# Picked pairs, feature products and prologue of a graph-and-expert kernel: products issued in halves, bias as three bfloat16 parts, zero rows by transfers, first lists per tile

## The reference, cut to what matters

```python
def _graph_conv_max(x, src, dst, W_rel, b, W_root):
    agg = jax.ops.segment_max(x[src], dst, num_segments=N)
    agg = jnp.where(jnp.isfinite(agg), agg, 0.0)
    return agg @ W_rel.T + b + x @ W_root.T
...
    h = jax.nn.relu(_graph_conv_max(x, src, dst, W1_rel, b1, W1_root))
    h = jax.nn.relu(_graph_conv_max(h, src, dst, W2_rel, b2, W2_root))
...
    x = x + _L0_gnn_ref(_layernorm(x, axis=-1), edge_index, ...)
    x = x + _L0_ffn_ref(_layernorm(x, axis=-1)[None], ...)[0]
```

## Time and profile before

| what | value |
|---|---|
| median of 3 runs | 1110.98 us (1107.28 to 1113.2) |
| the profiled execution, its own time | 1114.74 us |
| its span, first to last instruction | 1112.9 us |
| busy share: PE, DVE, POOL, ACT | 70%, 65%, 56%, 25% |
| granted PE clock, mean | 0.86 of full |

### The profile page before, as it was taken

One profiled execution on the slowest core, in us unless ns is written; L12 is line 12 of the kernel. 1 busy time (PEld: TensorE's weight loads), 2 busy tenths in 40 slices (PEclk: granted clock), 3 DMA queues, 4 the chain that ended last, 5 costly groups with the idle time before them and its releaser, 6 DMA issues.

```text
span 1112.9 us, 14709 instructions
## 1 busy us (share of the span) xinstructions
PE 779.7 (70%) x3119; PEld 438.7 (39%) x3119; DVE 719.8 (65%) x1428; ACT 278.6 (25%) x527; POOL 619.3 (56%) x609
## 2 busy tenths in 40 slices
PE   0248148888888779757128898878788686958497
PEld 0133013333333333222016656646456463726243
DVE  4949848568655866681466765765757566657767
ACT  0274332213231222001002233223223131313132
POOL 6540365355545655761777777777777777720012
PEclk9869569899988889888567999989989788978889
DMA  4830666575556566757667888888887878855874
GB/s 129 287 109 1 237 181 184 166 222 155 159 178 210 154 188 213 210 161 255 195 194 209 289 255 274 256 263 246 274 276 237 262 236 257 271 169 204 331 313 173
DMA packets 116373, 238.75 MB, mean 215 GB/s; under 512 B 53464, under 2 KB 57836, under 8 KB 112475
## 3 DMA queue, kind: packets, MB, share of 16 engines
q0 software_dynamic: 46080, 149.94, 43.4%
q1 hardware_dynamic: 54536, 40.85, 12.2%
q10 hardware_dynamic: 15730, 47.66, 11.5%
HBM read 201.28 MB, written 42.63 MB: 219 GB/s over the span
## 4 chain that ended last, share of the span: by engine, by line
PE 21%; DVE 21%; DMA 20%; issue 17%; POOL 10%; ACT 4%; DVEq 3%; ACTq 3%; POOLq 2%; SPq 0%
DMA mem<-tab,ic 13%; POOL mem L828 9%; PE pp L1154 6%; DMA ic<-idxf 4%; PE prow L1074 4%; PE pl L1101 3%; DVE mem L1456 2%; DVE weights L895 2%; DVE acc L949 2%; DVE acc L884 2%; PE prow L1088 1%; PE prow L1072 1%; DVE mem L562 1%; PE prow L1064 1%; PE pp L1121 1%
## 5 line engine op out<-in xcount | busy, mean ns | idle before, releaser
L828 POOL DMA_INDIRECT mem<-tab,ic x524 | 542.9, 1036 | 278.7 <-issue 144.2
L949 DVE TENSOR_TENSOR acc<-acc,mem 128x512 f32<-128x512 f32 x338 | 223.2, 694 | 165.7 <-SPq L791 156.2
L1121 PEld LDWEIGHTS pp<-xnT,weights 128*128 128x128 f32 x1280 | 159.3, 205 | 9.8 <-issue 9.8
L884 DVE TENSOR_TENSOR acc<-acc,pp 128x1024 f32<-128x1024 f32 x90 | 109.5, 1217 | 77.9 <-PE pp L1154 75.1
L1121 PE MATMUL pp<-xnT,weights 128*128 128x128 f32 x1280 | 159.8, 288 | 0.0
L1132 PE MATMUL pp<-weights,mem 128*128 128x512 f32 x320 | 142.6, 593 | 0.9 <-ACT mem L1292 0.9
L1154 PE MATMUL pp<-weights,LT 128*128 128x512 bf16 x300 | 77.0, 409 | 51.8 <-ACT idxf L699 34.9
L895 DVE TENSOR_TENSOR weights<-weights,mem 128x1024 f32<-128x1024 f32 x83 | 101.8, 1227 | 8.5 <-DVE weights L895 5.8
L1154 PE MATMUL pp<-weights,slots 128*128 128x512 bf16 x300 | 73.0, 392 | 23.1 <-DVE acc L884 23.1
L1088 PE MATMUL prow<-weights,aggT 128*128 128x512 f32 x152 | 82.6, 694 | 8.5 <-ACT aggT L1250 7.8
L1273 ACT ACTIVATE mem<-pp,b1T 128x128 f32<-128x128 f32 x160 | 45.6, 368 | 168.3 <-PE pp L1121 163.6
(11 more groups left out here) (305 smaller groups left out, 849.6 us busy)
## 6 DMA issues: line engine op xcount, KB each, us to landing
yd<-mem ACTq DMA_DIRECT2D x20, 1024.0 KB
weights<-yd SPq DMA_DIRECT2D x10, 2048.0 KB, 10.5
mem<-tab,ic POOLq DMA_INDIRECT x524, 3.9
weights<-in_L_ffn_W SPq DMA_DIRECT2D x9, 512.0 KB, 9.4
weights<-in_L_ffn_W ACTq DMA_DIRECT2D x7, 512.0 KB, 4.9
LT<-ttd ACTq DMA_DIRECT2D x5, 640.0 KB, 7.0
slots<-ttd ACTq DMA_DIRECT2D x5, 640.0 KB, 7.7
ic<-idxf SPq DMA_DIRECT2D x175, 1.0 KB
```

The lines of the kernel that those rows point to most:

```text
L828: g.indirect_dma_start(rings[l][:, j, :], None, table, bass.IndirectOffsetOnAxis(ic[:, j:j + 1], 0)).then_inc(s_gather[j], 16)
L884: v.tensor_tensor(acc[:, :, :], acc[:, :, :], pp[j % 2][:, :, :], ALU.max).then_inc(S["pa"], 1)
L949: v.tensor_tensor(acc[:, side, :], acc[:, side, :], rings[l][:, bass.ds(r % SLOTS, 1), :].rearrange("p a d -> p (a d)"), ALU.max).then_inc ...
L1121: ins = t.matmul(ph[w % 2][:, b * P:b * P + P], w1s[:, e, c, f * P:f * P + P], xnT[:, c, :], start=c == 0, stop=c == C - 1)
```

## The change

1. In layer 1, `root_product` is split: its transposes stand alone (`root`), and its product and `next_root_product` come in halves of two feature chunks, with one pair between the halves. `neighbours_product` comes after pair 6 instead of after pair 4.
2. The biases, formerly a float32 row times a row of ones, are cut into three bfloat16 parts by POOL (one cast and one subtraction in turn), laid on three partitions by three POOL DMAs, and added by one bfloat16 matmul.
3. POOL's memset of `hot`'s partitions 96 to 127 goes; partitions 125 to 127 are written by four transfers of the ACT queue at the start.
4. DVE's moments of `x` come after the ranks instead of before.
5. PE no longer waits for ACT's last instruction of the prologue, and SP loads the first index columns after the first of the ten lists (POOL still waits for all ten).

```diff
+        brow = acc[0:1, :, :]
+        bias3, ones3 = sb("bias3", [3, 2, D], BF16), sb("ones3", [3, P], BF16)
...
+        after(a, cg, n_neg)
+        zeros = zrow.bitcast(BF16).unsqueeze(1)
+        a.dma_start(hot[CN:CN + 1, :, 0, :], negrow.unsqueeze(1).to_broadcast([1, NC, D])).then_inc(S["neg"], 16)
+        a.dma_start(hot[CN:CN + 1, :, 1:3, :].rearrange("p c w d -> p c (w d)"), zeros.to_broadcast([1, NC, 2 * D]))\
+            .then_inc(S["neg"], 16)
+        for r in range(CN + 1, P):
+            a.dma_start(hot[r:r + 1, :, :, :].rearrange("p c w d -> p (c w d)").rearrange("p (i d) -> p i d", d=2 * D),
+                        zeros.to_broadcast([1, 3 * NC // 2, 2 * D])).then_inc(S["neg"], 16)
...
         for q in range(NQ):
+            if q == NQ - 1:
+                g.wait_ge(S["small"], 64)
             g.indirect_dma_start(big_rows[:, q, :], None, dstf,
...
-        after(g, cg, cg.n)
-        n_hot0 = cg.do(g.memset(hot[96:P, :, :, :], 0.0))
+        cg.do(g.memset(ones3[:, :], 1.0))
+        cg.link(g.tensor_copy(bparts[0], brow))
+        cg.link(g.tensor_tensor(brow, brow, bparts[0], ALU.subtract))
+        cg.link(g.tensor_copy(bparts[1], brow))
+        n_bias = cg.link(g.tensor_tensor(bparts[2], brow, bparts[1], ALU.subtract))
+        for i in range(3):
+            g.dma_start(bias3[i:i + 1, :, :], bparts[i]).then_inc(S["bias"], 16)
...
-        v.wait_ge(S["x"], 64)
-        cv.link(v.memset(mv[:, :, :], 1.0))
-        for q in range(NQ):
-            cv.do(v.bn_stats(st[0:CN, q, :], big_x[0:CN, q, :]))
...
+        v.wait_ge(S["x"], 64)
+        cv.link(v.memset(mv[:, :, :], 1.0))
+        for q in range(NQ):
+            n = cv.do(v.bn_stats(st[0:CN, q, :], big_x[0:CN, q, :]))
...
-        after(t, ca, ca.n)
         after(t, cv, n_meta)
         after(t, ca, n_low[NC - 1])
-        t.wait_ge(S["neg"], 16)
+        t.wait_ge(S["neg"], 64)
+        t.wait_ge(S["bias"], 48)
...
-            after(s, ca, n_idxf if l else n_idx1)
+            after(s, ca, n_idxf if l else n_idx1s[0])
...
                 def pe_tile(q, u):
                     pairs(q, u, (0, 1))
-                    root_product(q - 1)
+                    root(q - 1)
                     pairs(q, u, (2,))
+                    root_product(q - 1, (0, 1))
+                    pairs(q, u, (3,))
+                    root_product(q - 1, (2, 3))
                     neighbours(q - 1)
-                    pairs(q, u, (3, 4))
+                    pairs(q, u, (4, 5, 6))
                     neighbours_product(q - 1)
-                    pairs(q, u, (5, 6))
+                    pairs(q, u, (7,))
                     next_root(q - 1)
-                    pairs(q, u, (7, 8, 9))
-                    next_root_product(q - 1)
+                    pairs(q, u, (8,))
+                    next_root_product(q - 1, (0, 1))
+                    pairs(q, u, (9,))
+                    next_root_product(q - 1, (2, 3))
```

More of the change, by code:

```diff
@@ L221, in build @@
             ob oe od gd bn rc hs nmx exp apart_s warm apart_g apart_v x2l y out
-            neg bits pairs pa ga merge""".split()
+            neg bits bias pairs pa ga merge""".split()
         S = {n: sem("s_" + n) for n in names}
@@ L431, in build @@
         after(a, cg, n_neg)
-        after(a, cg, n_hot0)
-        a.dma_start(hot[CN:CN + 1, :, 0, :], negrow.unsqueeze(1).to_broadcast([1, NC, D])).then_inc(S["neg"], 16)
         after(a, cv, n_mean)
@@ L784, in build @@
                     .then_inc(S["fw"], 16)
+            else:
+                after(s, ca, n_idx1)
             def landed(i, h):
@@ L1065, in four, with root, root_product @@
                 ins.then_inc(S[event], 1)
-            def root_product(q):
+            def root(q):
                 t.wait_ge(S["rin"], q + 1)
                 four(pt0, xin, "rT")
-                t.wait_ge(S["rTe"], q + 1)
-                t.matmul(pg, ones[0:1, :], brow[0:1, 0, :], start=True, stop=False)
-                for c in range(C):
+            def root_product(q, cs):
+                if cs[0] == 0:
+                    t.wait_ge(S["rTe"], q + 1)
+                    t.matmul(pg, ones3[:, :], bias3[:, 0, :], start=True, stop=False)
+                for c in cs:
                     t.matmul(pg, rootT[:, c, :], wroot[0][:, c, :], start=False, stop=False)
@@ L1094, in next_root, with next_root_product @@
                 four(pt1, hst, "hT")
-            def next_root_product(q):
-                t.wait_ge(S["hTe"], q + 1)
-                t.matmul(pl[:, :], ones[0:1, :], brow[0:1, 1, :], start=True, stop=False)
-                for c in range(C):
+            def next_root_product(q, cs):
+                if cs[0] == 0:
+                    t.wait_ge(S["hTe"], q + 1)
+                    t.matmul(pl[:, :], ones3[:, :], bias3[:, 1, :], start=True, stop=False)
+                for c in cs:
                     ins = t.matmul(pl[:, :], xnT[:, c, :], wroot[1][:, c, :], start=False, stop=c == C - 1)
-                ins.then_inc(S["rp"], 1)
+                if cs[-1] == C - 1:
+                    ins.then_inc(S["rp"], 1)
             def ffn(q, between):
@@ L1174, in build @@
                 pe_tile(NQ - 1, 1)
-                root_product(NQ - 1)
+                root(NQ - 1)
+                root_product(NQ - 1, range(C))
                 neighbours(NQ - 1)
@@ L1178, in build @@
                 next_root(NQ - 1)
-                next_root_product(NQ - 1)
+                next_root_product(NQ - 1, range(C))
             else:
```

7 lines of the change are left out of this document (5 added, 2 removed).

## The result

The kernel with the change took 1075.91 us (median of 4 runs, 1074.5 to 1077.1), the kernel before 1111.32 us (1107.28 to 1113.2, its three runs and a fourth taken beside the change). The ratio is 0.9686, with a 95% interval of 0.9656 to 0.9716. The prediction was 1073 us within 1057 to 1091. On some chips single executions of one kernel differ by over 1.5%; ratios and intervals are taken from those that lie within that of the fastest, and where too few were left no ratio is given.

The account below looks back on a forecast made before the run. No engine is full (PE 70%), so waits decide, chiefly DVE's 74.4 us for pairs on PE. Terms -6.6, -7.5, -20.4, -3.6 sum to -38.1: 1114.74 becomes 1076.6, or 1073 us against the median, range 1057 to 1091.

Parts of the forecast that it names:

- tile 0, with the lists: Layer 1's first tile: earlier index columns and no PE wait for ACT's last list, less gather limits and cold start; -7.5 us.
- tiles 1 to 9: Layer 1: third pair waits for nothing, short waits remain at pairs 3, 4, 9; 54 us of waits for 74.4, -20.4 us.
- tail: After tile 9: root product and bias run bare, `xin` 2.0 us sooner, bias 0.4 instead of 2.05; -3.6 us.
- The key: Prologue, DVE's L363: without the memset it shortens by up to 8.6 us, less 2 for POOL's bias work; gain 6.6.
- What is late next is PE: Prologue: PE's transposes of the counts end at 104.5 instead of 106.06, so L588 moves from 111.30 to about 104.7.
- The lists: Tile 0: index columns loaded after the first list let POOL's first gather start at 139.2 instead of 141.51; 2.3 us.
- (a): Rival, layer 1: waits only move, both halves run at 1.2 GHz, tiles 1 to 9 gain next to nothing; 1093 us, chance 0.17.
- (b): Rival, prologue: POOL's bias work holds DVE as the memset did, until 37 us, so no gain there; 1080 us, chance 0.08.
- (c): Rival: all waits go and DVE runs through in tiles 1 to 9 and the prologue; 1055 us, chance 0.08.
- (d): Rival, slower: PE kept at 1.2 GHz becomes the bound, 54 us a tile against 36.4; 1250 us, chance 0.03.
- (e): Rival: POOL still waits for the tenth list and something unseen holds PE as before, no change; 1109 us, chance 0.02.
- The risk named for tiles 6 to 9: Sign of being wrong: DVE waits for SP's gathers in place of PE; 186 gathers need 232 of some 350 us.

Follow-up runs that it names:

- The kernel with the early copy: Changed kernel with ACT copying the next tile's `xin` at the end of the tile before, ahead of its wait for the root product: 1073.26 us, ratio 0.9636.
- the order alone: Kernel before with only PE's new order of layer 1, float32 bias kept; on three slower chips: 1296.53, 1294.75, 1288.84 us, third ratio 0.9835.
- the last experiment: Changed kernel with early `xin` copy, whole root product before pair 2, whole next root product before pair 7; three slower chips: 1279.31, 1273.38, 1268.23 us.

## Why the prediction was right, point by point

The prologue ends here with the last list (138.97 before, 135.06 with the change); its 3.9 us and 0.3 for the lists make the 4.2 by which the first fold came sooner.

| part | predicted | bounds | measured |
|---|---|---|---|
| prologue | -6.6 | -3 to -8.6 | -3.9 |
| tile 0, with the lists | -7.5 | -4 to -10.4 | -6.7 |
| tiles 1 to 9 | -20.4 | -36.6 to +2.1 | -23.9 |
| tail | -3.6 | -2 to -4 | -2.5 |
| layer 2 and last stage | 0 | -3 to +3 | -3.3 |
| sum | -38.1 | | -40.2 |

The sum is off by 2 us against the profiled executions and by 2.7 against the medians (35.4 us for 38.1), less than its parts are. The prologue, the lists and the tail fell short by 2.7, 2.0 and 1.1 us; tiles 1 to 9 and the rest of tile 0 gave 3.5 and 1.2 more, and layer 2 with the last stage 3.3 that was not forecast. That these cancel is luck; the mechanism in layer 1, which is the largest part, was right.

**The key** was right: 6.3 us instead of 6.6, and POOL held it for one instruction. I had allowed 2 us for that, and 2.3 were lost: the key took 1.97 us where its neighbours take 0.17, and L372 ahead of it 0.67 instead of 0.17. The prediction quoted the Trainium skill ("GPSIMD Engine Reference", "Elementwise — side-by-side cycle accounting") for an estimate of 2.2 us for each subtraction, and the trace agrees with 2.11. What it concluded from that, a gain some 2 us smaller, is wrong: only the last subtraction lay in the key's way, and the first one cost L372 0.5 us.

**The rest of the prologue** was mis-sized. "What is late next is PE" failed: PE's counts were ready at 104.2 and L605 read them at 107.52, behind DVE's own chain. The step priced that chain by the records, and left out that the gathers behind them share the DMA engines with the table's write, which hangs on the mean (1.2 us earlier) and not on the records (5.6 earlier). From the row that reads the sources to L588 or L605 it takes 32.78 us in both, so the whole loss lies ahead of it. L588 (now L605) stands at 107.52 instead of the 104.7 I expected, 3.8 gained. The kernel with the moments first shows the link: its records came 0.5 us later than the change's, and its sources were read 1.2 us earlier, with the write 3.8 earlier.

**The lists**, a part of tile 0: 0.3 us instead of 2.3. The step priced the wait for the last list and took the transfer as before, although the DMA engines were busy until 135 us. What remained of tile 0 was a little better than expected: 6.35 us from the first fold, where the cold start cost 1.67 us of waits (0.33 and 1.34) and I had taken 3 from a gain of 8.1.

**Tiles 1 to 9** were right in kind and near in size. The predicted waits are there. At full clock, where the sum had 1.3, 1.4 and 1.5 at pairs 3, 4 and 9, tile 9 has 1.45, 1.09 and 1.50, together 4.0 instead of 4.2. In tile 4 they are 2.30, 1.09 and 1.45, since pair 2 ran at 1.2 GHz, and in tile 5, the one worked out, 3.09, 1.09 and 1.44. I charged 54 us for all waits; they came to 47.5. Against the 26.9 us less of waits for pairs stand 23.9 gained: DVE's waits for gathers (L917, L915) rose from 16.4 to 20.2 us in all; that POOL is asked sooner would explain it, and is not tried. "`xin` and PE's transposes come 2 us sooner" was right: in tile 5 the transposes start 4.07 us behind the fold of the maximum (291.16 to 295.23) instead of 6.19, and 4.15 had been worked out. PE's wait for `xin` stayed at 15.9 us all the same, since PE's own work in front of it ended sooner too. The kernel with the early copy shows that this wait mattered little, since DVE's fold of pair 0 stood right behind it. And the halves, which the prediction took as the means, weren't needed: whole products behind pair 2 leave the same sum of waits.

The bias's share, which the prediction did not give apart, is some 1 to 1.5 us a tile by the runs of the order alone.

**The tail**: the bias took 0.60 us instead of 2.07, and PE and ACT were done 4.9 us sooner behind the maximum, more than the 3.6 predicted; then the last scatter took 5.12 us to land instead of 2.72. The loads of the experts' weights, issued over 13.42 us from 468.89, are beside it; the last of them was issued by 483.7, 2.4 us ahead of the scatter, where before it was issued by 518.0, 7.5 us ahead. That they slow the landing is argued, not tried.

**Layer 2** took 0.4 us less and the last stage 2.9 less. The same 300 matmuls there were busy for 87.9 us instead of 90.1, at a granted clock of 0.86 instead of 0.84. The change doesn't touch this stage, and why the clock differed wasn't found.

**Rivals.** (a) was wrong in that the third pair's place, not the halves' clock, decides. (b), a hold until 37 us, did not happen. (c) would have needed PE's hole filled, and the last experiment shows such a tile at 28.3 us. (d): tiles 1 to 9 ran at a granted clock of 0.93, far from the 0.72 where PE would bound. (e) didn't happen. The risk named for tiles 6 to 9, waits for gathers, is there in small: 3.8 us over all nine.

## What to carry to other kernels

Where an engine waits long for one product among many, move a small piece of what it needs ahead of the large piece; cutting the large one into halves only spreads the wait. When a wait is removed, look for the one right behind it on the same instruction: here `xin`, and then the PSUM tile of pair 0, came free about 1.2 us apart. Before you count an earlier issue of a transfer as a gain, look at what the DMA engines carry at that time, and at whether the data that lands last hangs on another chain.

## What the runs showed that I had not expected

A transfer of one index block, 1 KB, took 6.43 us to land when issued behind gathers and loads that kept the DMA engines busy, and 1.84 us when issued 4.6 us later: both landed at 136.4.

On three chips the same kernel was some 18% slower. Little of that is in the prologue (the key 8.70 and 8.75, L588 at 113.1 against 111.3, the first fold at 153.6 against 146.7) or in layer 1: the order alone on the third chip took 318.2 us for tiles 1 to 9, the kernel before on the fast one 328.4. Behind the maximum of tile 9 it took 782.6 us there and 609.3 on the fast chip, and PE stood idle for 112.6 us in front of one group of the expert products (0.0 on the fast chip), with nothing named that it waited for. No run here shows the cause.
